# Attention outputs kept with head dims on partitions, divided four pairs at a time, with a reordered lead-in, in a fused attention and feed-forward layer

## What is computed

```python
scores = jnp.einsum('bhid,bhjd->bhij', q, k) / jnp.sqrt(jnp.float32(hd))
std_out = out_proj(jax.nn.softmax(jnp.where(mask, scores, neg), axis=-1))
gsa_scores = scores + position_sensitivity * splat_attn
gsa_out = out_proj(jax.nn.softmax(jnp.where(mask, gsa_scores, neg), axis=-1))
blend = jnp.minimum(jnp.float32(0.03), jax.nn.sigmoid(gsa_strength) * 0.15)
return (1.0 - blend) * std_out + blend * gsa_out
...
x = _layernorm(x + _L0_attn_ref(...))
x = _layernorm(x + _L0_ffn_ref(x, ...))
```

## Time and profile before

| | |
|---|---|
| median of 3 runs | 402.3 us (401.74 to 403.64) |
| the profiled execution | 403.28 us, of which the span is 401.5 us |
| granted TensorE clock, mean | 0.987 of full |
| TensorE busy (PE) | 382.3 us, 95% |
| VectorE busy (DVE) | 307.2 us, 77% |
| ScalarE busy (ACT) | 231.2 us, 58% |
| GpSimd busy (POOL) | 125.9 us, 31% |

### The profile page before, as it was taken

One profiled execution on the slowest core, in us unless ns is written; L12 is line 12 of the kernel. 1 busy time (PEld: TensorE's weight loads), 2 busy tenths in 40 slices (PEclk: granted clock), 3 DMA queues, 4 the chain that ended last, 5 costly groups with the idle time before them and its releaser, 6 DMA issues.

```text
span 401.5 us, 6713 instructions
## 1 busy us (share of the span) xinstructions
PE 382.3 (95%) x2234; PEld 253.3 (63%) x2234; DVE 307.2 (77%) x900; ACT 231.2 (58%) x451; POOL 125.9 (31%) x173
## 2 busy tenths in 40 slices
PE   7996999999999999999999999999879899999995
PEld 7674658565565665665565565664435488888884
DVE  2779489998899798798899889887014457999955
ACT  4865243575676666676675776676774827443100
POOL 8578773203302212312312311473495200000000
PEclk9999699999999999999999999999998999999999
DMA  7142665100540450450450458000000000000003
GB/s 211 30 100 43 102 103 92 14 0 5 85 76 4 76 85 4 78 84 0 73 92 2 66 97 306 14 2 0 5 0 2 0 2 0 2 1 0 2 0 105
DMA packets 12906, 19.69 MB, mean 49 GB/s; under 512 B 5492, under 2 KB 8564, under 8 KB 12872
## 3 DMA queue, kind: packets, MB, share of 16 engines
q1 hardware_dynamic: 10328, 18.18, 22.8%
q0 software_dynamic: 1536, 1.07, 1.5%
q10 hardware_dynamic: 1008, 0.02, 0.1%
HBM read 5.26 MB, written 1.05 MB: 16 GB/s over the span
## 4 chain that ended last, share of the span: by engine, by line
PE 84%; DVE 6%; ACT 4%; POOL 3%; DMA 2%; issue 1%; SPq 1%; DVEq 0%; ACTq 0%
PE ps L961 19%; PE ps L935 17%; PE ps L900 17%; PE ps L861 7%; PE ps L763 6%; PE ps L765 6%; PE ps L764 6%; DVE ps L1260 3%; PE ps L922 2%; PE ps L825 2%; ACT pr L711 2%; DMA x_sb<-_attn_hidden_states_dram 1%; PE ps L845 1%; POOL wu_lo L548 1%; DVE mpart L1253 1%
## 5 line engine op out<-in xcount | busy, mean ns | idle before, releaser
L711 ACT ACTIVATE pr<-ps 128x512 f32<-128x512 f32 (+2 forms) x320 | 157.2, 561 | 80.5 <-PE ps L961 79.2
L1260 DVE CUSTOM_DVE_ANT_0 ps<-ps,causal 128x512 f32<-128x512 f32 (+3 forms) x256 | 145.8, 615 | 21.4 <-PE ps L900 19.6
L961 PE MATMUL ps<-q_st,k_st 67*128 67x512 f32 (+7 forms) x384 | 126.8, 373 | 0.3
L900 PE MATMUL ps<-k_st,q_st 65*128 65x512 f32 (+5 forms) x384 | 116.5, 359 | 1.8 <-DVE mpart L1260 1.3
L961 PEld LDWEIGHTS ps<-q_st,k_st 67*128 67x128 f32 (+1 forms) x384 | 68.0, 190 | 67.9 <-ACT pr L711 42.4
L935 PE MATMUL ps<-pr,vx 128*32 128x512 f32 (+3 forms) x768 | 82.5, 502 | 1.1 <-ACT o_sb L697 1.1
L557 POOL TENSOR_SCALAR_AFFINE_SELECT pr<-pr 128x512 f32<-128x512 f32 x64 | 40.7, 637 | 116.5 <-ACT pr L711 116.5
L900 PEld LDWEIGHTS ps<-k_st,q_st 115*128 115x128 f32 (+1 forms) x384 | 68.3, 191 | 13.9 <-DVE mpart L1260 5.5
L1253 DVE TENSOR_REDUCE mpart<-ps 128x1 f32<-128x384 f32 (+2 forms) x96 | 55.0, 597 | 8.4 <-PE ps L900 8.3
L1260 DVE DVE_READ_ACCUMULATOR2_ANT mpart<- 128x1 f32 x256 | 36.2, 141 | 0.0
L935 PEld LDWEIGHTS ps<-pr,vx 128*32 128x32 f32 x768 | 15.2, 108 | 23.7 <-ACT pr L711 13.3
(11 more groups left out here) (190 smaller groups left out, 496.6 us busy)
## 6 DMA issues: line engine op xcount, KB each, us to landing
q_st<-base_hiq SPq DMA_DIRECT2D x28, 64.0 KB
k_st<-base_hik SPq DMA_DIRECT2D x28, 64.0 KB
q_st<-feat_hiq SPq DMA_DIRECT2D x28, 64.0 KB
k_st<-feat_hik SPq DMA_DIRECT2D x28, 64.0 KB
x_sb<-_attn_hidden_states_dram SPq DMA_DIRECT2D x4, 256.0 KB, 4.7
raw<-in_L_ffn_w_gate_dram SPq DMA_DIRECT2D x1, 1024.0 KB, 4.8
raw<-in_L_ffn_w_up_dram SPq DMA_DIRECT2D x1, 1024.0 KB, 7.9
wd<-in_L_ffn_w_down_dram SPq DMA_DIRECT2D x1, 1024.0 KB, 9.9
```

The lines of the kernel that those rows point to most:

```text
L711: act.activation(pr[:, s % NP, 2 * hh + vs[0]:2 * hh + vs[-1] + 1, d:BANK], src, ACT.Exp, scale=SCALE).then_inc(exp_done, 1)
L900: mm = pe.matmul(ps[:, slot, at:at + n], q_st[b][0:rows, hh, i * P:(i + 1) * P], k_st[b][0:rows, hh, first:first + n], start=(v == v0), st ...
L961: mm = pe.matmul(ps[:, bank, j * width:(j + 1) * width], k_st[b][0:rows, hh, kt * P:(kt + 1) * P], q_st[b][0:rows, hh, q:q + width], start ...
L1260: ins = dve.tensor_tensor_reduce(out=ps[:, slot, at:at + n], in0=ps[:, slot, at:at + n], in1=causal[:, BANK - n:BANK], scale=1.0, scalar=- ...
```

## The change

The values of a pair get another layout in `vx`: ones, head 0, head 1, ones. The outputs of pairs 0 to 6 are no longer turned. SyncE sends them from `o_sb` to `outs`, where a partition is one dim of one head: six transfers for each pair and group, the outputs (kind 0) and the sums (kind 1) of both variants, the sums repeated over the 16 dims. The new VectorE item `norm` (`blended`) divides them: (0, g) for pairs 0 to 3 on 128 partitions, (1, g) for pairs 4 to 6 on 96. `halves` splits the result. Only pair 7 is still turned, and its 32 columns are turned back by `turn_last`. Up to step 83 `values` is called for two steps at a time, on odd steps. In the lead-in the reads of `wt` and `bt` come earlier, and `gauss` and `dirp` of the second half are spread one by one among the maxima. GpSimd fills the constants of the third operand buffer later.

```diff
-    A_LATER = ([("wt", 2), ("wt", 3)] + [("proj", 1, w, hf) for w in range(2) for hf in range(2)] + [("bt", 1)]
+    A_LATER = ([("wt", 2), ("wt", 3), ("proj", 1, 0, 0), ("bt", 1), ("proj", 1, 0, 1), ("proj", 1, 1, 0), ("proj", 1, 1, 1)]
...
-    UNIT = 6
-    for n, it in enumerate(late):
...
+    queue = guided0[n0:] + first_items(1, False) + first_items(1, True)
+    chunk1 = [use(k, *f) for f in features[TPG:] for k in ("gauss", "dirp")]
+    UNIT = len(queue) // len(chunk1)
+    for n, it in enumerate(queue):
...
-        if g == 1 and kt == 2:
+        if p == PPC and (g, kt) in ((0, 0), (1, 6)):
+            here.append(("norm", 0, g))
+        if p == PAIRS - 1 and kt == 1:
+            here.append(("norm", 1, g))
+        if p == PAIRS - 1 and g == 1 and kt == 2:
             here.append(("turn_out", p, 0))
         if p == PAIRS - 1 and g == 1:
 
-            here += {3: [("at", 0), ("at", 1)], 4: [("wo", 0), ("wo", 1)], 7: [("yt", 0), ("yt", 1)]}.get(kt, [])
-        if g == 0 and kt == 3 and p > 0:
-            here.append(("turn_out", p - 1, 1))
+            here += {3: [("at", 0)], 4: [("wo", 0), ("wo", 1)], 7: [("yt", 0), ("yt", 1)]}.get(kt, [])
...
+            def outputs(p, g):
+
+                sp.wait_ge(o_evac, G * p + g + 1)
+                if p >= PPC:
+                    sp.wait_ge(normed, g + 1)
+                row = 2 * HD * (p % PPC)
+                for v in range(2):
+                    first = 4 * HD * v
+                    for kind, at, src, n in ((0, row, first + HD, 2 * HD), (1, row, first, HD),
+                                             (1, row + HD, first + 3 * HD, HD)):
+                        sp.dma_start(outs[at:at + n, g, v, kind, :], o_sb[src:src + n, g, :]).then_inc(out_moved[g], 16)
...
             for p in range(PAIRS):
+                if p < PAIRS - 1:
+                    outputs(p, 0)
                 if p + 3 < PAIRS:
...
+                if p < PAIRS - 1:
+                    outputs(p, 1)
...
-            for b in range(1, NB):
-                constant_rows(b)
+            constant_rows(1)
...
             maxima(0)
+            constant_rows(2)
...
-                    act.wait_ge(ring_full, ring_at[("turn_out", (n - 2) // G, n % G)] + 1)
+                    act.wait_ge(out_moved[n % G], 16 * 6 * (n // G))
...
+            def turn_last(bank):
+
+                for t in range(TPG):
+                    mm = pe.matmul(ps[P - 2 * HD:P, bank, t * P:(t + 1) * P], own_out[:, t, :], ident[:], start=True, stop=True)
                 return mm
...
                 for it in mine:
-                    item(it)
-                if s >= PV_LAG:
+                    if it[0] != "yt":
+                        item(it)
+                if s < last_steps:
+                    if s % 2 == 1 and s >= PV_LAG + 1:
+                        values(s - PV_LAG - 1)
+                        values(s - PV_LAG)
+                else:
                     values(s - PV_LAG)
+                for it in mine:
+                    if it[0] == "yt":
+                        item(it)
...
+            def blended(c, g):
+
+                n = P if c == 0 else P - 2 * HD
+                dve.wait_ge(out_moved[g], 16 * 6 * (PPC if c == 0 else PAIRS - 1))
+                link(dve.reciprocal(outs[0:n, g, :, 1, :], outs[0:n, g, :, 1, :]))
+                for v in range(2):
+                    ins = dve.scalar_tensor_tensor(out=outs[0:n, g, v, 0, :], in0=outs[0:n, g, v, 0, :],
+                                                   scalar=blend[0:n, 0, v, 0:1], in1=outs[0:n, g, v, 1, :],
+                                                   op0=ALU.mult, op1=ALU.mult)
+                link(ins)
+                dve.tensor_tensor(heads_out[0:n, g, c, :], outs[0:n, g, 0, 0, :], outs[0:n, g, 1, 0, :],
+                                  ALU.add).then_inc(normed, 1)
+
+            def halves(g):
+
+                dve.wait_ge(normed, G + g + 1)
+                cols = slice(BANK * g, BANK * (g + 1))
+                for c, n in ((0, P), (1, P - 2 * HD)):
+                    ins = dve.tensor_copy(at_hi[0:n, c, cols], heads_out[0:n, g, c, :])
+                link(ins)
+                for c, n in ((0, P), (1, P - 2 * HD)):
+                    dve.tensor_tensor(at_lo[0:n, c, cols], heads_out[0:n, g, c, :], at_hi[0:n, c, cols].bitcast(F32),
+                                      ALU.subtract)
```

More of the change, by code:

```diff
@@ L175, in build_kernel @@
     vector_items = before + [it for here in at_step for it in here] + after
-    ring = [it for it in vector_items if it[0] not in ("rows", "a", "d", "mul", "lo")]
+    ring = [it for it in vector_items if it[0] not in ("rows", "norm", "a", "d", "mul", "lo")]
     ring_at = {it: r for r, it in enumerate(ring)}
     last_steps = (PAIRS - 1) * SPP
-    few = len(ring) - len([it for here in at_step[last_steps:] + [after] for it in here if it[0] != "rows"])
+    few = len(ring) - len([it for here in at_step[last_steps:] + [after] for it in here if it[0] not in ("rows", "norm")])
     ring_bank = [r % NR if r < few else r % (NR // 2) for r in range(len(ring))]
@@ L313, in build_kernel @@
         attn_done = sem("attn_done")
+        out_moved = [sem(f"out_moved{g}") for g in range(G)]
+        normed = sem("normed")
         reused = [sem(f"reused{b}") for b in range(NB)]
@@ L604, in high_half @@
         def high_half(act, kind, b, bank):
-            dst, t = (at_hi, 2 * P * (b % 2)) if kind == "at" else (yt_hi, 2 * P * b)
-            return act.activation(dst[:, :, t:t + 2 * P], ps[:, bank, :].rearrange("p (k t) -> p k t", k=KC), ACT.Copy)
+            if kind == "at":
+                return act.activation(at_hi[P - 2 * HD:P, 1, BANK * b:BANK * (b + 1)], ps[P - 2 * HD:P, bank, :], ACT.Copy)
+            return act.activation(yt_hi[:, :, 2 * P * b:2 * P * (b + 1)],
+                                  ps[:, bank, :].rearrange("p (k t) -> p k t", k=KC), ACT.Copy)
         @block.scalar
@@ L837, in _, with turn_tiles @@
                 opening_use(n)
-            def turn_tiles(kind, b, bank):
-                src = attn if kind == "at" else y
+            def turn_tiles(b, bank):
                 for k in range(KC):
@@ L849, in project_out @@
                 for j in range(2):
[L850 removed]
+                    tok = slice(P * (2 * b + j), P * (2 * b + j + 1))
                     for k in range(KC):
@@ L966, in _ @@
             for s in range(len(steps)):
-                mine = list(at_step[s])
+                mine = [it for it in at_step[s] if it[0] != "norm"]
                 for t in range(len(parts[s])):
@@ L1189, in low_half @@
             def low_half(kind, b, bank):
-                hi, lo = (at_hi, at_lo) if kind == "at" else (yt_hi, yt_lo)
-                t = 2 * P * (b % 2 if kind == "at" else b)
-                return dve.tensor_tensor(lo[:, :, t:t + 2 * P], ps[:, bank, :].rearrange("p (k t) -> p k t", k=KC),
-                                         hi[:, :, t:t + 2 * P].bitcast(F32), ALU.subtract)
+                if kind == "at":
+                    dims, cols = slice(P - 2 * HD, P), slice(BANK * b, BANK * (b + 1))
+                    return dve.tensor_tensor(at_lo[dims, 1, cols], ps[dims, bank, :], at_hi[dims, 1, cols].bitcast(F32),
+                                             ALU.subtract)
@@ L1224, in _ @@
                     opening_read(it[1])
+                    continue
+                if it[0] == "norm":
+                    blended(it[1], it[2])
+                    if it[1] == 1:
+                        halves(it[2])
                     continue
```

113 lines of the change are left out of this document (64 added, 49 removed).

## The result

| | before | after |
|---|---|---|
| median | 402.2 us (401.74 to 403.64, 4 runs) | 413.9 us (413.01 to 414.9, 4 runs) |
| profiled execution, span | 403.28, 401.5 us | 414.34, 412.5 us |
| mean granted TensorE clock | 0.987 | 0.957 |

The ratio is 1.0286, 95% interval 1.0249 to 1.0322: slower, by more than predicted, and above the predicted range (384 to 412 us). The sign was right. In all that follows medians are of all runs, while a ratio leaves out runs more than 1.5% above the fastest of their kernel.

A forecast was written before the change was run, and what follows sets the result against it. TensorE was taken to set the pace in the steps, with VectorE 3.8 us to spare in each pair. Terms summed to +2.6 us on the profiled 403.28, 405.9; being 1.0 above the median, 405 us was predicted, range 384 to 412.

The forecast's parts named there:

- values merged: Steps 3 to 83: 41 blocks of two steps each save TensorE 0.30 us; −11.0 us in all, bounds 0 and −14.
- turning leaves TensorE: Outputs no longer turned on TensorE: 0.65 us for each turn_out, 13 of 14 in stretches TensorE bounds; −8.4 us.
- waits for the ring in the steps: Steps (1, 2) to (1, 5): TensorE waits 0.35 us a pair for the four banks VectorE releases; +2.5 us (0 to 5).
- the divisions in pair 4, with the clock: Two norms of 9.0 us stall TensorE 8.5 and 7.0 us, +15.5; lower clock after each wait, 2 us each, +4.0.
- lead-in: Before the steps: earlier read of bt removes TensorE's 3.79 us wait and VectorE's 5.22 us idle time; −4.5 us.
- last pair: Last pair: norm(1, 1) and halves delay turn_out(7, 0), so at and wo start later; +6.0 us.
- small gains behind: Behind the last pair's wait: one turn_out, eight turnings in the feed-forward part, values ahead of yt; −1.5 us.
- Rivals 1 and 3: Reciprocal length: 1 said cheap, 1.05 ns an element, 384 us, chance 0.22; 3 said dearer, 8.3 ns, 410 us, 0.11.
- rival 4: Steps: merged blocks save nothing, since each step's values pay the fixed cost; 416 us, chance 0.05.
- rival 2: Reciprocal as dear as forecast, but the clock holds and the ring doesn't wait in the steps; 398 us, chance 0.12.

The follow-up runs named there:

- old_lead: Changed kernel with the lead-in of the kernel before (its order of reads, constants filled ahead of the maxima): 421.5 us, ratio 1.0447.
- compact_lead13: Changed kernel with each sum sent once for 64-element reciprocals, products and halves in the last pair, and 13 maxima ahead of the steps, not 10: 386.9 us.
- light_max: Changed kernel with VectorE's maxima taken over half of the columns only, so the output is another: 401.2 us, ratio 0.9969.
- unmerged: Changed kernel with values called in every step again, all else kept: 431.6 us, ratio 1.0604.
- unmerged_short: Changed kernel with values called in every step and reciprocals of 16 elements in the four divisions (another output): median 411.3 us, ratio 0.9998.
- late_last: Changed kernel with the division of group 1 of pairs 4 to 6 and its halves moved behind yt in the last pair: 419.5 us, ratio 1.0424.

## Where the prediction was right and where wrong

The two profiled executions differ by 11.06 us. TensorE's times in the steps can be read block by block, so each term has its measured counterpart. The first three are prices of one pair times 6.7. That factor is fitted: the steps outside the divisions took 10.9 us less in all, and a pair 1.62 less. So that the sum closes is no check of it; the share of each term rests on the prices.

| term of the sum | predicted | measured | from |
|---|---|---|---|
| values merged | −11.0 | −10.6 | 1.58 x 6.7 |
| turning leaves TensorE | −8.4 | −7.3 | 1.09 x 6.7 |
| waits for the ring in the steps | +2.5 | +7.0 | 1.05 x 6.7 |
| the divisions in pair 4, with the clock | +19.5 | +20.1 | four intervals of blocks, 36.57 us; undisturbed 16.49 |
| lead-in | −4.5 | −4.25 | first block 73.55, old_lead 77.80 |
| last pair | +6.0 | +6.05 | from its first block to the first gate matmul: 36.90, before 30.85 |
| small gains behind | −1.5 | 0 | feed-forward part 81.40, before 81.39 |
| sum | +2.6 | +11.0 | |

**The division was right.** The slope of 6.6 ns an element, taken from the rows of 1, 4 and 16 elements, measured 6.25, with a fixed 0.15 us: 6.55 us for 1024, 0.54 for 64, 0.25 for 16. Rivals 1 and 3 fall with that. The Trainium skill, "VectorE: DVE Perf Modes", walkthrough of the 8-slice pipeline, gives the reciprocal a repeat count of 8; read as eight slots of 1.05 ns that would be 8.4 ns, and the measurement, about six slots, decides against this reading. Each division stalled TensorE at its place as forecast (7.8 and 6.2 us against 8.5 and 7.0). The prediction's own sums are loose here: it adds 1.0 us for a maximum that it gives as 0.65, and with that the first wait is 8.15; the waits with a cheap reciprocal come to 4.1 and not 4.4. The clock cost 6.1 us, half of the 6.7 and 5.5 us that TensorE worked at 1.2 GHz behind the waits (to 203.4 and 237.5 us), and not 4.0. That the two together are within 0.6 us of the forecast is partly luck: waits 1.5 us too long and a clock 2.1 too cheap nearly cancel.

**Merging was right as a price.** It takes 0.26 to 0.29 us off TensorE for each pair of steps, forecast 0.30; rival 4 is out. The Trainium skill, "TensorEngine Tiling (Array Packing)", section Key Properties, says that a change of tiling mode drains TensorE. The measured gain fits a cost of the change of shape, paid once for a block of two steps; no run prices the drain by itself.

**The step that failed** is "Four banks hold some 2.5 us of VectorE's work (40 items in 25 us: 0.63 each), so I expect waits of 0.35 us in each pair: +2.5 us". They were 1.05 us, 7.0 us in all, which is 4.5 of the 8.5 us missing. The mean slack was there (3.1 us: VectorE has 24.9 of 27.99 us in compact_lead13), and without consequence: it lies in other steps. The prediction had named the right place, steps (1, 2) to (1, 5), where VectorE has as much to do as TensorE, but it priced it from means over a pair, where what decides is the run of VectorE's items in steps (1, 3) to (1, 5), `rows` and the short maxima, and the ring ahead of it, which VectorE has emptied by the end of the longer block of values. That this is so and not a lack of VectorE's time in all is shown twice: light_max removes the waits by less work, compact_lead13 by the same work three items earlier. So rival 2's ring that doesn't wait was within reach, but not in this order of items.

**Turning** was 1.09 us for two and not 1.30; why each was 0.1 us cheaper than its row in the trace of before had it was not looked into. **The small gains** were none: the feed-forward part is as long as before, and in it `turn_last` takes eight instructions of together 1.0 us, where the eight turnings of `at` took 0.8 (322.95 to 323.74 before, 334.04 to 335.03 after).

**The range** ended at 412. With all other terms as forecast and the ring's waits at their upper bound of 5 us the sum is some 408; the waits were 7.0, beyond that bound, and every other miss had the same sign, turning (1.1 us) and the small gains (1.5) above all.

What stays open: why the clock stayed at its lower level so much longer behind the same waits in `unmerged`, and what sets the clock in the longer runs of unmerged_short, old_lead and late_last. The runs show it, and none tells the cause.

## What to carry to other kernels

Where the second engine is busy for nearly 90% of the first one's time, as here, read its spare time step by step and not as a mean: part of what made the first one faster came back as waits where the second had its densest items. What helped then was where items stand: one number of the planner was worth 1.2 us a pair, twice what merging had given without it (0.53). A long operation on such an engine was paid for at both its places in pair 4 and at both places tried in the last pair; make it small before moving it, above all when its input holds the same number 16 times.
